# Softmax sums of the first attention layer as two rounded passes, placed one step later

## What is computed

```python
q = (layernorm(x) @ Wq)                        # 16 heads of 128
k, v = ctx @ Wk, ctx @ Wv                      # 8 heads, each used by two query heads
scores = einsum('bhtd,bhsd->bhts', q, k) / sqrt(128)
attn = softmax(scores, axis=-1)                # over 1500 keys
x = x + einsum('bhts,bhsd->bhtd', attn, v) @ Wo
```

## Time and profile before

| | |
|---|---|
| median of 3 runs | 2097.74 us (2097.26 to 2098.04) |
| profiled execution | 2097.64 us, its span 2095.9 us |
| PE / DVE / POOL / ACT busy, us | 2058.4 / 1578.0 / 1451.0 / 1208.0 |
| first layer's attention | about 75 to 1158 us of the span |
| first sum of a batch, first and last start | 145.4, and 1158.2 for the very last one |

### The profile page before, as it was taken

The page is one execution under the profiler, slowest core; times in us unless marked ns, Lnnn a source line. Parts: engine busy times, 40 slices in busy tenths (PEclk is TensorE's granted clock), DMA queues, the critical chain, the costliest instruction groups (busy, mean ns, idle before and its releaser), DMA issues. The chain is left out here.

```text
span 2095.9 us, 28195 instructions
## 1 busy us (share of the span) xinstructions
PE 2058.4 (98%) x8482; PEld 1525.9 (73%) x8482; DVE 1578.0 (75%) x2489; ACT 1208.0 (58%) x4201; POOL 1451.0 (69%) x1092
## 2 busy tenths in 40 slices
PE   7999999999999999999999899999999999999999
PEld 7877777777777777777777467666666666665998
DVE  4788988998889888898887766576766676752577
ACT  3576777767776777677777237544444444332432
POOL 1588888888888888988886145578787877851221
PEclk9999999999999999999999999999999999999999
DMA  3000000000000000000010410121111111101110
GB/s 137 30 16 16 31 30 16 26 19 31 30 16 15 30 31 15 22 24 30 26 41 1 152 41 1 45 59 30 59 30 59 32 57 42 33 0 53 46 47 25
DMA packets 15145, 75.68 MB, mean 36 GB/s; under 512 B 1746, under 2 KB 2114, under 8 KB 13986
## 3 DMA queue, kind: packets, MB, share of 16 engines
q1 hardware_dynamic: 14994, 73.89, 10.8%
HBM read 72.97 MB, written 0.92 MB: 35 GB/s over the span
## 5 line engine op out<-in xcount | busy, mean ns | idle before, releaser
L550 ACT ACTIVATE l_prod_act<-l_prod_act 125x128 f32<-125x128 f32 x1536 | 456.3, 299 | 298.6 <-DVE l_prod_act L734 293.5
L646 POOL TENSOR_TENSOR l_prod<-l_prod 125x256 f32<-125x256 f32 x384 | 280.3, 739 | 163.9 <-DVE l_prod L734 162.6
L999 POOL TENSOR_TENSOR l_acc<-l_acc,l_probs 125x896 f32<-125x896 f32 x160 | 346.6, 2167 | 67.9 <-ACT l_probs L936 49.6
L936 ACT ACTIVATE l_probs<-l_scaled 125x896 f32<-125x896 f32 x192 | 182.8, 952 | 302.7 <-DVE l_scaled L1021 160.5
L1021 DVE TENSOR_TENSOR l_scaled<-l_slots,rk 125x896 f32<-125x896 f32 x192 | 206.9, 1084 | 180.8 <-PE l_slots L1097 180.7
L640 POOL TENSOR_TENSOR l_acc<-l_acc,l_probs 125x896 f32<-125x896 f32 x160 | 339.8, 2124 | 0.0
L550 ACT ACTIVATION_READ_ACCUMULATOR l_prod_act<-l_prod_act 125x1 f32 x1536 | 287.8, 187 | 0.0
L710 DVE SCALAR_TENSOR_TENSOR top<-l_side,mask_bias,top 125x448 f32<-125x448 f32 x330 | 217.6, 659 | 25.7 <-PE l_side L822 17.6
L568 ACT ACTIVATE l_probs<-l_slots,mask_bias 125x448 f32<-125x448 f32 x384 | 219.6, 617 | 1.2
L1095 PE MATMUL l_slots<-l_qhi,l_clo 128*125 128x448 f32 x384 | 203.0, 529 | 0.4
L838 PE MATMUL l_side<-norm_lo,l_chi 128*125 128x512 f32 x384 | 185.2, 482 | 0.1
(11 more groups left out here) (270 smaller groups left out, 4964.7 us busy)
## 6 DMA issues: line engine op xcount, KB each, us to landing
land<-in_ctxT SPq DMA_DIRECT2D x32, 750.0 KB, 4.2
l_nat<-in_ctxN SPq DMA_DIRECT2D x16, 750.0 KB
post_we<-in_experts SPq DMA_DIRECT2D x20, 384.0 KB, 3.0
spare<-in_ctxN SPq DMA_DIRECT2D x8, 750.0 KB
nat<-in_ctxN SPq DMA_DIRECT2D x8, 750.0 KB
spare<-in_wo SPq DMA_DIRECT2D x2, 2048.0 KB, 7.4
spare<-in_wqT SPq DMA_DIRECT2D x4, 512.0 KB, 9.0
mid_fac<-in_factors SPq DMA_DIRECT2D x1, 2048.0 KB, 7.6
```

The lines of the kernel that those rows point to most:

```text
L550: last = act.activation(whole, whole, ACT.Copy, accum_out=msq[:, t, 4 * g + c:4 * g + c + 1])
L646: pool.tensor_tensor(buf[:, :, 0:C // 2], buf[:, :, 0:C // 2], buf[:, :, C // 2:C], ALU.add).then_inc(s.half_sum, 1)
L999: pool.tensor_tensor(acc[:, :], acc[:, :], P[t % NP][:, :], ALU.add).then_inc(s.acc, 1)
```

## The change

The sum of a batch is made from a high and a low part, as two fp32r matmuls with ones. ACT rounds `acc` into the idle query remainder `qlo[b % 2]` (`sum_high`), POOL puts the rest into the idle `shift[b % 2]` (`sum_low`), whose buffers and `ones_r` become larger. The sums move one step: half 0 into step 1, half 1 to the start of step 2. ORDER moves them behind S(2,.). On ACT the copies out move too: half 0 behind the `add_up` of the A block with i = 3, half 1 to the start of step 2. The last batch keeps its fp32 sum. `add` of tile 1 waits for `sum_lo` instead of the sum on PE, and the next users of the two buffers wait for the sums. Some semaphore increments elsewhere are dropped.

```diff
-ORDER = [("S", 0, 0), ("S", 0, 1), ("S", 1, 0), ("S", 1, 1), ("D", 0, 0), ("D", 0, 1), ("-", 0, 0)]
-ORDER += [("S", t, half) for t in range(2, NT) for half in range(2)]
+ORDER = [("S", t, half) for t in range(3) for half in range(2)] + [("D", 0, 0), ("D", 0, 1), ("-", 0, 0)]
+ORDER += [("S", t, half) for t in range(3, NT) for half in range(2)]
...
+            def sum_high(b):
+                act.wait_ge(s.acc, (NT - 1) * (b + 1))
+                act.wait_ge(s.scores, 2 * NT * (b + 1))
+                act.activation(qlo[b % 2][0:KT, :], acc[:, :], ACT.Copy).then_inc(s.sum_hi, 1)
...
+                    if t == 2 and b > 0:
+                        sums_out(b - 1, 1)
                     for tile in tile_ahead(1, b, t):
                         exp(*tile)
                     if t == 0 and b > 0:
-                        sums_out(b - 1, 0)
+                        sum_high(b - 1)
                         norms_out(b - 1)
...
                         if JOBS[n].kind == "A":
                             add_up(n)
-                        if n == first_of(b, "A") and b > 0:
-                            sums_out(b - 1, 1)
+                        if JOBS[n].kind == "A" and JOBS[n].i == 3 and b > 0:
+                            sums_out(b - 1, 0)
...
                 if b >= 2:
                     pool.wait_ge(s.scores, 2 * NT * (b - 1))
+                    pool.wait_ge(s.den, 2 * (b - 1))
...
                 if t == 1:
-                    need(pool, s.den, 2 * b)
+                    need(pool, s.sum_lo, b)
                     pool.tensor_tensor(acc[:, :], P[0][:, :], P[1][:, :], ALU.add).then_inc(s.acc, 1)
...
+            def sum_low(b):
+                pool.wait_ge(s.sum_hi, b + 1)
+                pool.tensor_tensor(shift[b % 2][:, :], acc[:, :], qlo[b % 2][0:KT, :].bitcast(F32), ALU.subtract).then_inc(s.sum_lo, 1)
...
                         if JOBS[n].kind == "N":
                             halve(n)
+                    if t == 0 and b > 0:
+                        sum_low(b - 1)
...
             def sums(b, half):
-                pe.wait_ge(s.acc, (NT - 1) * (b + 1))
+                cols, out = slice(HALF * half, HALF * half + HALF), bank_of("D", 0, half)[:, 0:HALF]
                 wait_bank(pe, b + 1, "D", 0, half)
-                pe.matmul(bank_of("D", 0, half)[:, 0:HALF], m.ones[0:KT, :], acc[:, HALF * half:HALF * half + HALF],
-                          start=True, stop=True).then_inc(s.den, 1)
+                if b == B - 1:
+                    pe.wait_ge(s.acc, (NT - 1) * B)
+                    pe.matmul(out, m.ones[0:KT, :], acc[:, cols], start=True, stop=True).then_inc(s.den, 1)
+                    return
+                pe.wait_ge(s.sum_lo, b + 1)
+                pe.matmul(out, m.ones_r[0:KT, :], shift[b % 2][:, cols], start=True, stop=False)
+                pe.matmul(out, m.ones_r[0:KT, :], qlo[b % 2][0:KT, cols], start=False, stop=True).then_inc(s.den, 1)
...
-                    if t == 1 and b > 0:
+                    if t == 2 and b > 0:
                         sums(b - 1, 1)
...
-                        if half == 1 and t == 0 and b > 0:
+                        if half == 1 and t == 1 and b > 0:
                             sums(b - 1, 0)
```

More of the change, by code:

```diff
@@ L309, in make_shift @@
                 dve.wait_ge(s.ld_ident, 16)
-                dve.tensor_tensor(m.shift0[:, :].rearrange("p (j c) -> p j c", c=TT),
+                dve.tensor_tensor(m.shift0[0:TT, :].rearrange("p (j c) -> p j c", c=TT),
                                   m.negmax[:, :].unsqueeze(2).to_broadcast([TT, QBLK, TT]),
@@ L442, in first_attention @@
         "ld_land", "ld_nat0", "ld_nat1", "ctx_hi", "ctx_lo", "q_hi", "q_lo", "nat_hi", "xq", "shift",
-        "scores", "probs", "pv", "acc", "den", "den_out", "inv", "o_raw", "o_done",
+        "scores", "probs", "pv", "acc", "sum_hi", "sum_lo", "den", "den_out", "inv", "o_raw", "o_done",
         "ld_wv", "ld_wo", "side_pe", "side_dve", "side_act", "half_sum", "sum_dve", "sum_act", "rk_pre"])
@@ L458, in first_attention @@
         top, negmax = m.top, m.negmax
-        shift = [m.shift0, sb("shift1", [TT, QW], F32R)]
+        shift = [m.shift0, sb("shift1", [KT, QW], F32R)]
         prod = [sb(f"prod{i}", [KT, 4, C], F32) for i in range(NPROD)]
@@ L667, in make_shift @@
                 need(pool, s.scores, 2 * NT * (b - 1))
-                pool.tensor_tensor(shift[b % 2][:, :].rearrange("p (j c) -> p j c", c=TT),
+                need(pool, s.den, 2 * (b - 1))
+                pool.tensor_tensor(shift[b % 2][0:TT, :].rearrange("p (j c) -> p j c", c=TT),
                                    negmax[:, :].unsqueeze(2).to_broadcast([TT, QBLK, TT]),
@@ L790, in scores_half @@
                 pe.matmul(out, chi[b % 2][:, keys], qhi[b % 2][:, cols], start=False, stop=False)
-                pe.matmul(out, m.ones_r[:, :], shift[b % 2][:, cols], start=False, stop=True).then_inc(s.scores, 1)
+                pe.matmul(out, m.ones_r[0:TT, 0:KT], shift[b % 2][0:TT, cols], start=False, stop=True).then_inc(s.scores, 1)
             def values_half(b, t, half):
@@ L872, in second_attention @@
         "ld_land", "ld_nat0", "ld_nat1", "ctx_hi", "ctx_lo", "q_hi", "q_lo", "scores", "scaled", "probs", "pv", "pv_first", "acc",
-        "acc_hi", "acc_lo", "den", "inv", "o_raw", "o_done", "fold_pe", "fold_act", "fold_dve", "y_pe", "y_act"])
+        "acc_hi", "acc_lo", "den", "inv", "o_raw", "o_done", "fold_pe", "fold_act", "fold_dve", "y_pe"])
     LAG, NP = 2, 3
@@ L981, in _ @@
                 act.wait_ge(s.y_pe, i + 1)
-                act.activation(land[:, HALF * i:HALF * i + HALF], slots[:, 0, i, 0:HALF], ACT.Copy).then_inc(s.y_act, 1)
+                act.activation(land[:, HALF * i:HALF * i + HALF], slots[:, 0, i, 0:HALF], ACT.Copy)
         @block.gpsimd
@@ L1242, in between_layers @@
     s = semaphores(sem, tag, ["ld_fac", "ld_bias", "ld_wq", "ld_wk", "ld_g", "ld_next", "ready", "on_act", "on_dve", "fac", "gain",
-                 "zero", "one_r", "bias", "rk_std", "rk_inv", "x_hi", "w_hi", "w_lo", "w_lo1", "sq", "sq_hi", "sq_lo", "ms", "std", "rinv", "r_hi", "r_lo"])
+                 "zero", "one_r", "bias", "rk_std", "x_hi", "w_hi", "w_lo", "w_lo1", "sq", "sq_hi", "sq_lo", "ms", "std", "rinv", "r_hi", "r_lo"])
     with ExitStack() as ctx:
@@ L1410, in _ @@
             for i in range(B):
-                dve.reciprocal(m.rk[:, i, :, :], m.rk[:, i, :, :]).then_inc(s.rk_inv, 1)
+                dve.reciprocal(m.rk[:, i, :, :], m.rk[:, i, :, :])
             for n in range(1, NWQ - 1, 2):
@@ L1941, in build @@
             for_first = lambda n, sh, dt: only.enter_context(nc.sbuf_tensor(n, sh, dt))
-            m.ones_r = for_first("ones_r", [TT, KT], F32R)
+            m.ones_r = for_first("ones_r", [C, C], F32R)
             m.mask_bias = for_first("mask_bias", [KT, B, NT], F32)
@@ L1949, in build @@
             m.top, m.negmax = for_first("top", [KT, QW], F32), for_first("negmax", [TT, QBLK], F32)
-            m.shift0 = for_first("shift0", [TT, QW], F32R)
+            m.shift0 = for_first("shift0", [KT, QW], F32R)
             m.xq = for_first("xq", [KT, NT, C], F32)
```

## The result

| | before | changed |
|---|---|---|
| median, us | 2097.53 (4 runs) | 2161.06 (4 runs, 2159.60 to 2161.83) |
| profiled execution, its span, us | 2097.64, 2095.9 | 2161.83, 2159.9 |
| mean granted clock | 0.996 | 0.983 |

The ratio is 1.0302, 95% interval 1.0284 to 1.0320: the changed kernel is 63.5 us slower. The forecast was slower by 35 us, with 2142 as the upper end.

The account below looks back on a forecast made before the run. PE's queue was taken as full, 67.6 of 67.68 us a batch. Fourteen batches at +2.29 us and the last at +2.9 gave +35 on 2097.64, so 2132.7 us, range 2118 to 2142.

Parts of the forecast that it names:

- upper end: Whole kernel: 2142 us, from all batches like the last (+2.9 us each) or a quarter of the stalls with a clock fall.
- The bound: First layer: PE's queue has no hole, 67.6 of 67.68 us a batch counted, so savings and waits go straight into time.
- Part 1: First-layer sums: two fp32r passes replace each fp32 product in fifteen batches, 0.69 us less on PE a batch, 10.4 in all.
- Part 2: First layer, steps 0 and 1: waits ahead of the sum's new place leave PE 0.62 us early a batch instead of 1.10.
- the right two waits: First layer: values(b,0) waits for psO, leaving 0.51 of 0.755 us; the sum waits for sum_low, starting 489.78 rather than 489.55.
- Part 3: First layer, step 2: S(3,0) waits for ACT's copy of sum half 0; PE stands 2.5 us, net +2.29 a batch.
- Part 4: Remaining waits, POOL and ACT work, memset and increments count nought; the last batch costs +2.9 us.
- Rival 3, the clock,: First-layer stalls also lower PE's clock, 1.7 us a fall: 2139.5 us for one in four, 2158 for all; chance 0.13.
- its case of all fifteen: All fifteen first-layer stalls bring a clock fall: +25.6 us, 2158 us.
- The argument against it: First layer: PE is dense on both sides of each stall, while only short matmuls preceded the 3.39 us idle that brought a fall.
- The row with 1.20 us: Trace before the change: after PE idled 1.20 us the clock stayed 1.00; after 3.39 us it was 0.50 for 3.4 us.
- The sign that I named for this: Profile page, slices 3 to 22: PEclk below 9 would refute the steady clock.

Follow-up runs that it names:

- e7: e4 with one fp32 product a half in place of the two fp32r passes, low part of the sums left out; 2103.44 us, ratio 1.0026.
- e4: Changed kernel with sum halves moved to the starts of steps 2 and 3, each copied out at the start of ACT's same step; 2092.84 us, ratio 0.9978.
- e5: e4 with psO emptied ahead of a batch's last add_up and two banks for the last batch's sums; 2087.89 us, ratio 0.9950.
- e1: Changed kernel with ACT copying both sums out ahead of the add_up of block 3; 2099.85 us, ratio 1.0010.
- e3: Changed kernel with eight more score passes (1.64 us of PE work) in step 6 of fifteen batches, stall kept; 2169.89 us, ratio 1.0343.
- e2: Changed kernel with only the copy of sum half 0 moved ahead of the add_up of block 3; 2119.29 us, ratio 1.0102.
- e6: Changed kernel with four more score passes (0.82 us of PE work) in step 6 of fifteen batches; 2160.48 us, ratio 1.0296.

## Why the prediction was wrong

- **The bound** (PE's queue without a hole) was right: e7 gives back 10.1 of 10.4 us, so reading headroom from the busy share of weight loads, as the Trainium skill has it (Perfetto Trace Analysis, Identifying the Most-Contended Engine), did not hold in this layer, with weight loads busy 75%. But what PE saves did not go straight into the time: even with the sums spread out, 0.31 of 0.69 us a batch arrived (e4), then 0.54 (e5).
- **Part 1** was right: 0.69 us a batch.
- **Part 2** had the right two waits and sized them low. Block 3 came 0.30 us early, not 0.62. values(b,0) began 1.00 after the end of S(1,1) where I had 0.91; POOL took up sum_low 0.70 after the start of its second halving as reckoned, but that began 0.16 later; and the sum's first pass started at 512.68, with its second 0.29 rather than 0.205 behind it. That is 15 x 0.32 = 4.8 us.
- **Part 3** was right to 0.04 us: from block 3 to S(3,0) 3.35 us against 3.39, and fifteen stalls released by ACT's copy. e1, which moves the copies and nothing else, shows it to be the cause. It takes stall and fall away together; that a fall needs more than such a stall comes from e3. The last batch has the stall too.
- **Part 4** was right: the list of PE's waits has no other kind in this layer.
- **Rival 3, the clock,** is the step that failed: 24 of the 28.5 us between forecast and result. The sum has no term for it, though the clock in fact fell at all fifteen stalls. Its price for a fall (1.7, measured 1.58) was close, and its case of all fifteen (2158 us) came within about 3 us, but I gave the rival a chance of 0.13 and took only a quarter of the stalls into the range. The argument against it, that PE is dense on both sides of the stall, weighed nothing: the clock fell all the same. The row with 1.20 us that I set against the 3.39 proved true for 1.03 (e2), but 2.3 was on the other side, and even 1.74 was at times. The sign that I named for this, PEclk below 9 in a slice, could not have come: a fall of 3.4 us in a slice of 54 leaves its mean at 0.97, and all forty digits stayed 9. The Trainium skill (TensorE: Matmul & The Clock Gate, HAM oscillation) has pauses in a loop bring a fall again and again; the changed kernel's trace agrees, with 15 in 15, and e3 and e6, with 4 and 7 in 15, show that it is no matter of the pause alone.
- What I left out is that the stalls do not meet the clock at random. I priced "a quarter" or "all", as if drawing lots. A batch with its fall is 71.7 to 71.9 us long and the falls come 71.68 apart, so a batch that fell brings the next one to the same place. Without a fall it would be 70.3, 1.4 off the beat, and the stalls would have gone through its places, some of which bring no fall (e3). The changed trace also shows the batch giving way to the beat: the first fall began 1.29 us after its restart (160.29), the thirteenth 0.39 before its own (1022.13), so that part of it lay inside the stall, and from 71.88 the batches had come down to 71.7. This holding of step is my reading of the times; e3 and e6, which broke it by adding work, bear it out, and no run shortens the batch with the stall left as it was.

The range ended at 2142 for the same reason: its upper end took a fall at a quarter of the stalls, or every batch as long as the last, and not a fall at all of them.

## What to carry to other kernels

When a step is moved, follow the buffer it fills to its next user, and look at what stands ahead of the copy that empties it in the other engine's program. Where PE will stand still at regular distances for as long as here (1.7 us or more), let the range reach from no fall of its clock to a fall at every stall: the counts here were 4, 7 and 15 of 15, and 0 of 15 at 1.03 us. Look for such falls in windows of a few microseconds, not in the slices of the page. A count of passes saved is worth only what remains after the two waits nearest to it; here they took it all, until the sums were put where nothing waits for them.

## What the hardware showed that I had not expected

- The granted clock fell to 0.50 for 3.4 us after stalls of 1.74 and 2.3 us between dense work, never after 1.03 us (0 of 15). A fall costs 1.6 us. Without a fall, a stall still makes the first pass behind it take 0.31 us instead of 0.205.
- Of stalls of the same 2.3 us, 15, 7 and 4 of 15 brought a fall in the profiled executions, as 0, 0.82 and 1.64 us of work were added to a batch 18 us behind the stall. The kernel with 12.3 us more work took 2160.5 us, the one without 2161.1.
